# Two preactivation convolutions over 8 images: 32x32 array tiles, four quarters of one image at a time, in place of 64x64 tiles on pairs of images

## The chip, the cores and the metric

The kernel runs on one core of a Trainium2 chip. The metric is the device time of one execution in microseconds. Three runs of the kernel before took 4153.45, 4162.24 and 4164.72 us, so its median is 4162.24 us.

## The reference

The input is `x`, 8 images of 8 channels of 1024 x 1024 float32 (33.6 MB an image). Two layers of the same form follow each other:

```
x = x + conv3x3(groupnorm(x), L0_weight) + L0_bias
x = x + conv3x3(groupnorm(x), L1_weight) + L1_bias
```

The group norm has 4 groups of 2 channels, its mean and variance run over both channels and all rows and columns of one image, with eps 1e-5 and no affine part. The convolution has 8 input and 8 output channels, stride 1 and a border of one zero around the normalised image. Both layers stay in float32.

## The kernel before

**The idea.** The kernel never writes a normalised image. It multiplies the taps by 1/std of the input channel's group, adds the identity to the middle tap (that is the `x +` of the reference), puts what the mean contributes into the bias, and fills the border with the mean, which is zero once normalised. So a layer is one convolution with weights that are made anew for every image, after its mean and variance are known. The result of layer 0 goes to a scratch tensor in HBM, `mid`, and layer 1 reads it back.

**The tiling.** The contraction runs over rows and channels at once: a band matrix maps 8 input rows x 8 channels (64 partitions) to 6 output rows x 8 channels. Horizontal taps are three matmuls that read the same rows shifted by a column (`kw`), added up in PSUM. The TensorE array is used as four 64x64 tiles. In layer 0 (`convolve`, line 620 and on) the two halves of the partitions hold two images and the two column groups two bands of 6 rows; in layer 1 it is the other way round. Neighbouring bands overlap by two rows, so layer 0 loads 8 rows for every 6 that it computes; in layer 1 the overlap is copied inside SBUF by GpSimd (line 405) and ScalarE (line 508).

**The work.** A unit is 12 rows of two images: 24 program matmuls of 512 columns, each of which stands in the trace as two pairs of weight load and matmul (33,232 matmul records; 32,832 of them for the convolutions, from 16,416 in the program). A window is one layer of one pair of images: 85 units and a last one of 4 rows. There are 8 windows, in the order of pairs and layers 0/0, 1/0, 0/1, 2/0, 1/1, 3/0, 2/1, 3/1, so that between the two layers of a pair another pair's window is at work. Of each window 56 units run in a loop (7 trips of 8 units), the others are written out.

**Who does what.** SyncE loads `x` a second time, in pieces of 1 MB, for its statistics (line 270), for the first pair ahead of everything and for the others beside the windows. VectorE takes `bn_stats` of these pieces (L700) and of layer 0's results (L710), makes the weights, and in layer 1 adds the bias to half of the results (L727). ScalarE takes the results out of PSUM (L465, L470) and issues the loads of a unit eight units ahead (L479 from `x`, L492 from `mid`). GpSimd issues the stores (L371 to `mid`, L385 to the output) and copies halo rows. A unit may start when its rows and borders are in SBUF and the results of two units earlier have left PSUM; a result may be written to `out_tile` when the store of four units earlier has landed.

## Time and profile before

| | |
|---|---|
| median of 3 runs | 4162.24 us (4153.45 to 4164.72) |
| span of the profiled execution | 4141.6 us; its time outside the span is not shown; the median run is 20.6 us above the span |
| TensorE matmul busy | 3666.7 us, 89%, 33,232 records |
| VectorE, ScalarE, GpSimd busy | 2025.6, 1762.8, 1360.0 us |
| mean granted TensorE clock | 0.983 |
| moved by DMA | 1435.04 MB, 346 GB/s over the span |
| first convolution matmul | 228.1 us after the start |

The span is one profiled execution. Busy time is the union of an engine's instructions. Four matmuls are at work on the four tiles at the same time, so the mean of one (598 ns) is not what one costs. The DMA row counts the share of time in which the 16 DMA engines had a packet under way, also where that packet waited for memory, so a 9 there does not say that no more bytes could pass; the GB/s row does.

### The profile page before, as it was taken

To read this page: it belongs to the slowest core of one execution; us is meant where nothing else is said; L and a number is where in the kernel's file an instruction comes from. 1 tells how busy PE (TensorE), PEld (TensorE's weight loads), DVE (VectorE), ACT (ScalarE), POOL (GpSimd) and SP (SyncE) were. 2 spreads that over 40 slices of the span, in tenths; PEclk is the share of its full clock that TensorE was granted. 3 is DMA by queue.
4 is the path that set the end of the run, shared out by engine and by line. 5 is a ranking of instruction groups with operands and counts; after the bars stand their busy time and mean duration, and the time that the engine had idled before them with its cause. 6 is when DMAs were issued, how large, how long until landed. Compare 5 with 4: busy or idle time off the path is not lost.

```text
span 4141.6 us, 88712 instructions
## 1 busy us (share of the span) xinstructions
PE 3666.7 (89%) x33232; PEld 1715.4 (41%) x33232; DVE 2025.6 (49%) x3110; ACT 1762.8 (43%) x1381; POOL 1360.0 (33%) x1829
## 2 busy tenths in 40 slices
PE   0087777898889999999888999999999999999999
PEld 0032222353334433354333443345444444566665
DVE  6866666665556344446656444444445322232222
ACT  0032222343334555543333555544443555555554
POOL 0011111121112555531111455552111455555555
PEclk9999998999999999999999999999999999999999
DMA  9989999999999999999999999999999999999997
GB/s 333 396 291 393 386 374 371 366 368 387 382 382 331 331 367 385 380 318 391 390 388 384 305 357 371 374 295 368 362 355 333 291 306 306 306 287 304 305 303 237
DMA packets 367109, 1435.04 MB, mean 346 GB/s; under 512 B 49888, under 2 KB 50016, under 8 KB 334176
## 3 DMA queue, kind: packets, MB, share of 16 engines
q10 hardware_dynamic: 176736, 627.30, 47.9%
q0 software_dynamic: 153344, 536.96, 34.5%
q1 hardware_dynamic: 36864, 268.45, 16.9%
q8 instruction: 119, 1.95, 0.2%
q14 instruction: 46, 0.38, 0.0%
HBM read 895.64 MB, written 536.87 MB: 346 GB/s over the span
## 4 chain that ended last, share of the span: by engine, by line
PE 56%; DMA 15%; ACTq 11%; issue 10%; DVE 5%; ACT 2%; DVEq 0%; POOL 0%; POOLq 0%; SPq 0%
PE conv L653 56%; DMA out_dram<-out_tile 12%; ACTq L479 11%; DMA stat_tile<-x_dram 2%; DVE bn_x L700 2%; ACT out_tile L465 1%; DVE bn_mid L710 1%; DMA mid_dram<-out_tile 1%; DVE out_tile L727 1%; DVE mv_mid L738 1%; DVEq L700 0%; DVE mv_x L732 0%; PE conv L555 0%; ACTq L461 0%; PE conv L583 0%
## 5 line engine op out<-in xcount | busy, mean ns | idle before, releaser
L653 PE MATMUL conv<-x_tile,wts 64*64 64x512 f32 x32832 | 3648.7, 598 | 235.5 <-ACT out_tile L465 140.4
L653 PEld LDWEIGHTS conv<-x_tile,wts 64*64 64x64 f32 x32832 | 1694.9, 134 | 2170.3 <-issue 2037.0
L465 ACT ACTIVATE out_tile<-conv,bias 128x1024 f32<-128x1024 f32 x688 | 728.6, 1110 | 1340.5 <-PE conv L653 791.1
L710 DVE BATCH_NORM_STATS2 bn_mid<-out_tile 128x512 f32 (+1 forms) x1376 | 849.3, 680 | 881.1 <-ACT out_tile L465 880.9
L727 DVE TENSOR_SCALAR out_tile<-conv,bias 128x1024 f32<-128x1024 f32 x340 | 436.4, 1284 | 1168.7 <-PE conv L653 856.7
L371 POOL DMA_DIRECT2D mid_dram<-out_tile x680 | 343.4, 507 | 1708.1 <-ACT out_tile L465 1641.4
L470 ACT ACTIVATE out_tile<-conv,bias 128x1024 f32<-128x1024 f32 x344 | 383.1, 1114 | 764.4 <-PE conv L653 505.6
L508 ACT ACTIVATE x_tile<-x_tile 16x2048 f32<-16x2048 f32 x340 | 648.6, 1908 | 44.9 <-issue 31.6
L700 DVE BATCH_NORM_STATS2 bn_x<-stat_tile 128x512 f32 (+1 forms) x1024 | 628.7, 678 | 45.6 <-DMA stat_tile<-x_dram 45.5
L405 POOL COPY x_tile<-x_tile 16x2048 f32<-16x2048 f32 x340 | 639.1, 1880 | 1.7
L385 POOL DMA_DIRECT2D out_dram<-out_tile x680 | 348.3, 514 | 823.7 <-DVE out_tile L727 758.8
L555 PE MATMUL conv<-share,average 128*128 128x8 f32 x32 | 5.5, 281 | 227.4 <-DVE share L746 222.3
L555 PEld LDWEIGHTS conv<-share,average 128*128 128x128 f32 x32 | 4.8, 215 | 233.3 <-issue 221.5
L396 POOL COPY x_tile<-pad 128x4 f32<-128x4 f32 x64 | 12.2, 198 | 173.2 <-DVE pad L821 172.1
L522 ACT ACTIVATE root<-var 128x8 f32<-128x8 f32 x8 | 1.7, 208 | 137.3 <-DVE var L790 137.2
L738 DVE BATCH_NORM_AGGREGATE mv_mid<-bn_mid 128x2 f32<-128x12 f32 (+1 forms) x24 | 40.1, 1698 | 0.0
L522 ACT ACT_TABLE_LOAD x1 | 1.3, 1283 | 84.5 <-issue 84.5
L732 DVE BATCH_NORM_AGGREGATE mv_x<-bn_x 128x2 f32<-128x192 f32 x32 | 29.9, 983 | 0.0
L335 POOL TENSOR_SCALAR own_group<-same_group 128x4 f32<-128x4 f32 x2 | 0.4, 188 | 44.0 <-DMA rows<-taps_dram 43.9
L379 POOL DMA_DIRECT2D out_dram<-out_tile x16 | 7.8, 495 | 13.4 <-ACT out_tile L470 13.4
L592 PEld LDWEIGHTS conv<-taken,band 64*64 64x64 f32 x144 | 7.2, 134 | 2.2 <-issue 2.2
L583 PE MATMUL conv<-taken,band 64*64 64x1 f32 x144 | 5.5, 208 | 2.7 <-DVE taken L818 2.7
(62 smaller groups left out, 114.5 us busy)
## 6 DMA issues: line engine op xcount, KB each, us to landing
x_tile<-x_dram ACTq DMA_DIRECT2D x680, 512.0 KB, 23.0
stat_tile<-x_dram SPq DMA_DIRECT2D x256, 1024.0 KB, 9.8
out_dram<-out_tile POOLq DMA_DIRECT2D x680, 384.0 KB, 7.8
mid_dram<-out_tile POOLq DMA_DIRECT2D x672, 384.0 KB, 9.3
x_tile<-mid_dram ACTq DMA_DIRECT2D x340, 640.0 KB, 6.4
x_tile<-mid_dram ACTq DMA_DIRECT2D x344, 128.0 KB, 8.5
mid_dram<-out_tile POOLq DMA_DIRECT2D x8, 416.0 KB, 10.0
x_tile<-x_dram ACTq DMA_DIRECT2D x8, 256.0 KB
```

What stands on the lines that cost most here:

```text
L371: pool.dma_start(mid[win.image + i, bass.ds(unit.n * OUT_ROWS + (CH - extra), OUT_ROWS + extra), :], out_tile[VALID - extra:VALID + OUT_RO ...
L385: pool.dma_start(pair[:, bass.ds(row, ROWS_OUT), :], out_tile[VALID:VALID + OUT_ROWS, slot, band]) \
L405: pool.tensor_copy(x_tile[0:PAIR, unit.slot, :, 1:SIDE + 1], x_tile[HALF:HALF + PAIR, earlier.slot, :, 1:SIDE + 1]) \
L465: last = act.activation(out_tile[0:parts, slot, i], conv[0:parts, bank, i], ACT.Identity, bias=bias0[0:parts, win.parity, int(unit.last), ...
L470: last = act.activation(out_tile[:, slot, 0], conv[:, bank, 0], ACT.Identity, bias=bias1[:, win.parity, unit.kind:unit.kind + 1])
L479: act.dma_start(x_tile[:, slot, band, 1:SIDE + 1], rows.rearrange("n c r w -> (n c) r w")) \
L508: act.activation(x_tile[HALF + HALF // 2:HALF + HALF // 2 + PAIR, unit.slot, :, 1:SIDE + 1], x_tile[HALF // 2:HALF // 2 + PAIR, unit.slot, ...
L653: last = nc.tensor.matmul(to, weights, x_tile[HALF * half:HALF * (half + 1), slot, middle, c + kw:c + kw + BANK], start=(kw == 0), stop=(k ...
L700: last = dve.bn_stats(bn_x[:, bass.ds(t * STAT_PARTS + q, 1), :].rearrange("p a b -> p (a b)"), stat_tile[:, s, q * BANK:(q + 1) * BANK])
L710: last = dve.bn_stats(bn_mid[0:parts, unit.win.pair % 2, i, bass.ds(unit.n * 2 + h, 1), :] .rearrange("p a b -> p (a b)"), out_tile[0:part ...
L727: dve.tensor_scalar(out_tile[:, slot, 1], conv[:, bank, 1], bias1[:, win.parity, INNER:INNER + 1], None, ALU.add) \
L738: return dve.bn_aggr(mv_mid[:, region, i, :], bn_mid[:, of.pair % 2, i, first:end, :] .rearrange("p a b -> p (a b)"))
```

## The change

It is a rewrite of the tiling with the same arithmetic idea.

- The array is used as sixteen 32x32 tiles. The four row groups of 32 partitions hold the same rows of four quarters of one image (256 rows each), 4 rows x 8 channels in a partition group. The four column groups are four successive blocks of 4 output rows. The loaded rows are shifted by one against the computed rows, so an output block of 4 rows needs its own block of 4 loaded rows and the next one, and no row is loaded twice.
- An output block is therefore six matmuls (two parts, MAIN and NEXT, by three `kw`) of 32x32 weights. Each row group adds up in a PSUM bank of its own; half the columns (512) of a unit fill four of the eight banks.
- A unit is now 16 rows of each quarter, 64 rows in all: 192 program matmuls. There are 16 units a layer of one image, 256 in the whole kernel (49,152 program matmuls).
- Layers 0 and 1 of an image follow each other directly, and images are taken one by one. Only the next image's statistics run beside the current image. Layer 1 begins with the statistics of all of layer 0's results.
- Image 0 and image 7 are written out, images 1 to 6 run in a loop whose body is a whole image.
- GpSimd issues all loads of `x` (16 of 128 KB a unit) and all stores of the output (16 of 128 KB a unit). SyncE issues the stores to `mid` (4 of 512 KB), the loads from it (4 of 512 KB) and the statistics' loads. ScalarE issues none and takes all results out of PSUM, four banks at a time. No halo is copied.
- `x_tile` and `out_tile` are rings of 4 units of 2 MB each.

The sizes, and in `STATS_0` and `STATS_1` which of the next image's 32 statistics pieces are loaded beside which unit:

```diff
-X_RING = 8
...
-PAIRS = IMAGES // 2
...
+QUARTERS = 4
+QUARTER = SIDE // QUARTERS
+TILE = P // QUARTERS
+BLOCKS = 4
+BLOCK_ROWS = 4
+UNIT_ROWS = BLOCKS * BLOCK_ROWS
+UNITS = QUARTER // UNIT_ROWS
...
+X_RING = 4
...
+STATS_0 = ((0, 1, 2, 3), (4,), (5,), (6, 7), (8,), (9,), (10,), (11, 12), (13,), (14,), (15,),
+           (16,), (17,), (18,), (19,), (20,))
+STATS_1 = ((21,), (22,), (23,), (24,), (25,), (26,), (27,), (28,), (29,), (30,), (31,),
+           (), (), (), (), ())
```

SyncE, one image:

```diff
+            def image(n):
+                win, after = Window(0, n), Window(1, n)
+                for u in range(UNITS):
+                    stats_of_next(win, u)
+                    store_mid(win, u)
+                    first = u - (UNITS - X_RING)
+                    if first >= 0:
+                        sp.wait_ge(stored[0][first % RING], stores_through(win, first))
+                        load_mid(after, first)
+                for s in range(RING):
+                    sp.wait_ge(stored[0][s], stores_through(win, UNITS - RING + s))
+                load_edge(after)
+                for u in range(UNITS):
+                    stats_of_next(after, u)
+                    if u + X_RING < UNITS:
+                        sp.wait_ge(conv_done, HALVES * (after.g + u + 1))
+                        load_mid(after, u + X_RING)
...
```

GpSimd, the loads of `x` and the units of layer 1:

```diff
+            def load_x(n, u):
+                for j in range(BLOCKS):
+                    for q in range(QUARTERS):
+                        row = QUARTER * q + UNIT_ROWS * u + BLOCK_ROWS * j - 1
+                        if row >= 0:
+                            pool.dma_start(x_tile[TILE * q:TILE * (q + 1), u % X_RING, j, 1:SIDE + 1],
+                                           x_block(n, row)).then_inc(rows_loaded[0][u % X_RING], 16)
...
+                for u in range(UNITS):
+                    store_out(after, u)
+                    if not after.last_image and u >= UNITS - X_RING:
+                        load_x(n + 1, u - (UNITS - X_RING))
+                        if u == UNITS - 2:
+                            pool.wait_ge(pad_known, after.w + 2)
+                            pool.sem_inc(results_seen)
+                            load_edge(n + 1)
+                            for s in range(X_RING - 1):
+                                write_pads(0, s)
+                if not after.last_image:
+                    write_pads(0, X_RING - 1)
+                    load_tail(n + 1)
```

TensorE (inside the loop over the two halves `c` of the columns and the two parts), and ScalarE, which takes four banks at a time:

```diff
-                        for half in range(1 if unit.last and win.layer else 2):
-                            for middle in range(1 if unit.last and not win.layer else 2):
...
-                                last = nc.tensor.matmul(
-                                    to, weights,
-                                    x_tile[HALF * half:HALF * (half + 1), slot, middle,
-                                           c + kw:c + kw + BANK],
-                                    start=(kw == 0), stop=(kw == KW - 1))
...
+                        for kw in range(KW):
+                            at = c * BANK + kw
+                            for j in range(BLOCKS):
+                                here = u * BLOCKS + j + part
+                                for q in range(QUARTERS):
+                                    rows = slice(TILE * q, TILE * (q + 1))
...
+                                    last = nc.tensor.matmul(
+                                        conv[TILE * j:TILE * (j + 1), c, q],
+                                        wts[rows, win.layer, part, kw], moving,
+                                        start=(part == MAIN and kw == 0),
+                                        stop=(part == NEXT and kw == KW - 1))
...
+                act.activation(out_tile[:, slot, :, c * BANK:(c + 1) * BANK], conv[:, c],
+                               ACT.Identity, bias=bias[:, win.layer:win.layer + 1]) \
+                   .then_inc(evicted, 1)
```

On TensorE, at the start of the first window, before (`x_loaded3` is the slot of the ring that holds the rows of the unit after the current one, `evicted_a` says that a result has left PSUM):

```order
L653 MATMUL conv<-x_tile,wts 64x512 [waits x_loaded2,pads_written]
L653 MATMUL conv<-x_tile,wts 64x512 x7
L653 MATMUL conv<-x_tile,wts 64x512 [waits evicted_a]
L653 MATMUL conv<-x_tile,wts 64x512 x15
L653 MATMUL conv<-x_tile,wts 64x512 [waits x_loaded3,pads_written]
L653 MATMUL conv<-x_tile,wts 64x512 x7
L653 MATMUL conv<-x_tile,wts 64x512 [waits evicted_a]
```

And the same place now:

```order
L534 MATMUL conv<-x_tile,wts 32x512 [waits x_loaded2,pads_written]
L534 MATMUL conv<-x_tile,wts 32x512 x47
L534 MATMUL conv<-x_tile,wts 32x512 [waits evicted]
L534 MATMUL conv<-x_tile,wts 32x512 x95
L534 MATMUL conv<-x_tile,wts 32x512 [waits evicted]
L534 MATMUL conv<-x_tile,wts 32x512 x47
L534 MATMUL conv<-x_tile,wts 32x512 [waits x_loaded3,pads_written]
```

24 matmuls of 64 rows stood between two waits for loaded rows, now 192 of 32 rows do.

On GpSimd, at the end of layer 1 of the first image and the beginning of the next, now (before, GpSimd issued two stores a unit there and loaded nothing):

```order
L309 DMA out_dram<-out_tile 8x4x1024 x208
L322 DMA x_tile<-x_dram 32x1x1024 x15
L309 DMA out_dram<-out_tile 8x4x1024 x16
L322 DMA x_tile<-x_dram 32x1x1024 x16
L309 DMA out_dram<-out_tile 8x4x1024 x16
L322 DMA x_tile<-x_dram 32x1x1024 x16
L327 TENSOR_SCALAR x_tile<-zeros,own_mean 32x1024
L332 DMA x_tile<-x_dram 8x1024 x3
L352 COPY x_tile<-pad 128x4x2 x3
L309 DMA out_dram<-out_tile 8x4x1024 x16
L322 DMA x_tile<-x_dram 32x1x1024 x16
```

The next image's border rows and pads (L332, L352) stand behind the stores of units 12 to 14 and the loads of the next image's units 0 to 2.

## Rows read from the trace of the kernel before

**Rows 1.** The page: busy time of the engines, and their shares in 40 slices.

```profile
PE 3666.7 (89%) x33232; PEld 1715.4 (41%) x33232; DVE 2025.6 (49%) x3110; ACT 1762.8 (43%) x1381; POOL 1360.0 (33%) x1829
...
PE   0087777898889999999888999999999999999999
...
GB/s 333 396 291 393 386 374 371 366 368 387 382 382 331 331 367 385 380 318 391 390 388 384 305 357 371 374 295 368 362 355 333 291 306 306 306 287 304 305 303 237
```

**Rows 2.** Waits of TensorE: total us, times, longest.

```profile
PE conv L653 <- ACT out_tile L465: 140.4, 64, 5.0
PE conv L653 <- DMA x_tile<-x_dram: 41.5, 31, 2.9
PE conv L653 <- DVE out_tile L727: 39.3, 31, 3.1
```

**Rows 3.** Windows: PE, PEld, DVE, ACT, POOL busy, clock, DMA share, GB/s.

```profile
0.00:120.00 120.00, 0.00 (x0) 0.00 (x0) 76.10 (x126) 1.28 (x1) 6.86 (x41) 1.00 1.00 330
120.00:218.00 98.00, 0.00 (x0) 0.00 (x0) 94.70 (x152) 0.00 (x0) 0.00 (x0) 1.00 1.00 411
300.00:740.00 440.00, 346.60 (x2820) 124.81 (x2816) 283.46 (x471) 122.86 (x116) 59.57 (x118) 0.91 1.02 382
1880.00:2240.00 360.00, 318.02 (x2835) 128.84 (x2829) 216.40 (x358) 124.97 (x118) 60.04 (x120) 0.98 1.03 388
3360.00:3620.00 260.00, 260.00 (x2424) 122.96 (x2422) 64.69 (x51) 151.54 (x101) 146.83 (x151) 1.00 1.00 306
3580.00:3770.00 190.00, 190.00 (x1778) 117.14 (x1773) 64.76 (x86) 107.59 (x73) 105.28 (x118) 1.00 0.97 295
```

**Rows 4.** Timeline of weight loads, three places: start us, length us, count.

```profile
2000.70 0.18 PEld L653 LDWEIGHTS conv<-x_tile,wts 64*64 64x64 f32 x4 [0.25 <-issue]
2001.13 0.18 PEld L653 LDWEIGHTS conv<-x_tile,wts 64*64 64x64 f32 x4 [0.25 <-issue]
...
725.20 0.33 PEld L653 LDWEIGHTS conv<-x_tile,wts 64*64 64x64 f32 x8 [6.41 <-issue]
...
804.33 0.94 PEld L583 LDWEIGHTS conv<-taken,band 64*64 64x64 f32 x32 [0.30 <-issue]
```

**Rows 5.** Timeline at the start: the sums, then the first convolution.

```profile
220.38 0.17 DVE L746 COPY share<-mv_x 128x8 f32<-128x8 f32 x1
...
228.06 4.21 PE L653 MATMUL conv<-x_tile,wts 64*64 64x512 f32 x20 [0.68 <-DVE bias L846]
```

**Rows 6.** Groups by form: busy us, mean ns of one, idle before.

```profile
L700 DVE BATCH_NORM_STATS2 bn_x<-stat_tile 128x512 f32 x928 | 569.7, 678 | 45.6 <-DMA stat_tile<-x_dram 45.5
L738 DVE BATCH_NORM_AGGREGATE mv_mid<-bn_mid 128x2 f32<-128x1020 f32 x8 | 37.9, 4743 | 0.0
L732 DVE BATCH_NORM_AGGREGATE mv_x<-bn_x 128x2 f32<-128x192 f32 x32 | 29.9, 983 | 0.0
L465 ACT ACTIVATE out_tile<-conv,bias 128x1024 f32<-128x1024 f32 x680 | 720.2, 1110 | 1334.2 <-PE conv L653 784.8 <-issue 481.1 <-DMA mid_dram<-out_tile 45.0
```

**Rows 7.** Timeline of GpSimd: transfers issued back to back, loop and end.

```profile
3003.34 1.10 POOL L371 DMA_DIRECT2D mid_dram<-out_tile  x2 [3.96 <-ACT out_tile L465]
...
4135.05 1.95 POOL L379 DMA_DIRECT2D out_dram<-out_tile  x4 [4.02 <-ACT out_tile L470]
```

**Rows 8.** DMA issues of the page: count, KB each, median us to landing.

```profile
x_tile<-x_dram ACTq DMA_DIRECT2D x680, 512.0 KB, 23.0
out_dram<-out_tile POOLq DMA_DIRECT2D x680, 384.0 KB, 7.8
...
x_tile<-mid_dram ACTq DMA_DIRECT2D x344, 128.0 KB, 8.5
```

**Rows 9.** Instruction queue: in 1360 to 1362 us, then in 3580 to 3770.

```profile
q8 instruction: 1, 0.02, 3.9%
...
q8 instruction: 15, 0.25, 0.6%
```

More of the change, by code:

```diff
@@ L11 @@
 P = 128
-HALF = P // 2
 CH = 8
@@ L296, in _ @@
+            for i in range(STAT_SLOTS):
+                load_stat(0, i, None)
+            for i in range(STAT_SLOTS, STATS):
+                load_stat(0, i, i + 1 - STAT_SLOTS)
+            image(0)
+            with sp.Fori(1, IMAGES - 1) as n:
+                image(n)
+            image(IMAGES - 1)
+            last = Window(1, IMAGES - 1)
             for s in range(RING):
-                sp.wait_ge(stored[s], 32 * len(range(s, len(WINDOWS) * UNITS, RING)))
-            sp.wait_ge(stored_last, 16 * last_stores(len(WINDOWS)))
+                sp.wait_ge(stored[1][s], stores_through(last, UNITS - RING + s))
@@ new lines, in store_out @@
+            def store_out(win, u):
+                slot = u % RING
+                pool.wait_ge(evicted, HALVES * (win.g + u + 1))
+                pool.sem_inc(results_seen)
+                for q in range(QUARTERS):
+                    for j in range(BLOCKS):
+                        row = QUARTER * q + UNIT_ROWS * u + BLOCK_ROWS * j
+                        pool.dma_start(out[bass.ds(win.n, 1), :, row:row + BLOCK_ROWS, :]
+                                       .rearrange("n c r w -> (n c) r w"),
+                                       out_tile[TILE * j:TILE * (j + 1), slot, q]) \
+                            .then_inc(stored[1][slot], 16)
@@ L433, in _ @@
+            for u in range(X_RING):
+                load_x(0, u)
+            pool.wait_ge(pad_known, 1)
+            pool.sem_inc(results_seen)
+            load_edge(0)
+            for s in range(X_RING):
+                write_pads(0, s)
+            load_tail(0)
+            image(0)
+            with pool.Fori(1, IMAGES - 1) as n:
+                image(n)
+            image(IMAGES - 1)
         @block.scalar
@@ L549, in _ @@
+            take_root(0)
+            images(act, window)
         @block.tensor
         def _(pe):
-            def mean_sum(n, bank):
-                pe.wait_ge(mean_share, n + 1)
-                regions = 1 if WINDOWS[n].layer == 0 else 3
-                for region in range(regions):
-                    last = nc.tensor.matmul(conv[:, bank, 1, BANK:BANK + BOTH], average[:, :],
-                                            share[:, region], start=(region == 0),
-                                            stop=(region == regions - 1))
-                last.then_inc(mean_summed, 1)
@@ L560, in var_sum @@
-            def var_sum(n, bank):
-                pe.wait_ge(var_share, n + 1)
-                regions = 1 if WINDOWS[n].layer == 0 else 3
-                for region in range(regions):
-                    last = nc.tensor.matmul(conv[:, bank, 1, BANK:BANK + BOTH], average[:, :],
-                                            share[:, region], start=(region == 0),
-                                            stop=(region == regions - 1))
-                last.then_inc(var_summed, 1)
-            def own(i):
-                return slice(VALID * i, VALID * i + HALF)
```

1062 lines of the change are left out of this document (409 added, 653 removed).

## The prediction

> **What bounds the kernel now.** I first read the page's busy times and slices [rows 1]. TensorE is at work 89% of the span, and after the first twentieth, in which nothing but statistics is loaded, at 7 to 9 tenths. So TensorE sets the pace, but not alone: where its slices show 7 or 8, the GB/s row stands near 390, and where they show 9 throughout, at the end, near 305. The windows [rows 3] say the same in numbers. From 3360 to 3620 us TensorE is busy all 260 us at 306 GB/s; from 300 to 740 us only 346.6 of 440 us at 382 GB/s, from 1880 to 2240 us 318 of 360 at 388. The waits [rows 2] name the cause: 140.4 us for results that ScalarE could not take out because `out_tile` was not yet stored, 41.5 us for rows of `x`. I read from it that about 385 GB/s is what the mix of loads and stores gives, and 411 GB/s what pure loading gives (120 to 218 us). Both resources are thus nearly used up, and a change has to relieve both.
>
> Weight loads [rows 4] show the period of the array: four of them every 0.43 us at full clock, one for each tile. 32,832 records in fours are 8,208 periods, 3530 us of the 3649 that the convolutions take.
>
> **TensorE after the change.** 49,152 program matmuls, two records each, are 98,304; sixteen tiles at a time make 6,144 periods. A period streams the same 512 columns, so 0.43 us: 2642 us, or 10.3 us for each of the 256 units. That is 890 us less. The trace of before never has more than four tiles at work, so this has bounds. Below: 10.3 us. Above: no gain from more than four tiles, 41 us a unit. Two rows speak for the lower end. After a wait eight weight loads and their first matmuls go out within 0.33 us, and 32 weight loads of the bias sums pass in 0.94 us, 29 ns each [rows 4]; sixteen pairs at 29 ns are 0.47 us. I take 10.3 to 11.3 us a unit; it turns out not to matter, because of the next paragraph.
>
> **DMA after the change.** An image is 33.6 MB. It is read for its statistics, read for layer 0, written to and read from `mid`, and written out: 5 x 33.6 x 8 = 1342 MB, where 1435 MB moved before. At 385 GB/s that alone is 3486 us, so DMA is now the bound, and I sum by stages, for the images 0 to 6:
> - Layer 0: `x` for units 4 to 15 (25.2 MB), stores to `mid` (33.6), 21 of 32 statistics pieces (22.0), the first four units' rows of `mid` (8.4) are 89.2 MB, 232 us at 385 GB/s [rows 3], 14.5 us a unit, against 10.3 on TensorE.
> - From layer 0 to layer 1 nothing else can run on TensorE. Last results out: 1024 elements take 1110 ns, I put 2048 at 2.0; four `bn_stats` at 0.68 are 2.7; one aggregate of 768 elements at 4743/1020 ns each is 3.6 [rows 6]; from the shares to the first convolution 7.7 us [rows 5]. Sum 16 us. DMA still has stores and loads of its own in part of it, but stays nearly idle in unit 0 too, as loads wait for a slot and stores for results. I take 20 us for both.
> - Layer 1, units 0 to 11: 25.2 MB from `mid`, 25.2 stored, 11.5 of statistics, 61.9 MB, 161 us.
> - From unit 12 on GpSimd is the bound. Two issues stand 1.10 us long, four short ones 1.95 us [rows 7]: 0.49 to 0.60 us a transfer, I take 0.59. Behind unit 12's result stand 48 stores, 48 loads and 3 border rows before the next image may begin: 99 x 0.59 = 58 us, 4 us to land, and unit 12 itself 10.3: 72 us. TensorE would be through in 41.
>
> Sum 232 + 20 + 161 + 72 = 485 us, seven times 3395. The last image has no statistics beside it: 67.1 MB, 174 us; 16; sixteen units of TensorE, 165; the last result, 16 issues and the landing [rows 8], 19. Sum 374.
>
> The start: 32 pieces in place of 64 before the first matmul. 33.6 MB and 8.4 MB of `x` are 102 us at 411 and 127 us at 330 GB/s; VectorE needs 87 us for its 128 `bn_stats` [rows 3, 6]. I take 109, and 12 for four aggregates and the 7.7 us above: 121, where 228 stood [rows 5].
>
> 121 + 3395 + 374 = 3890 us. ScalarE (two results a unit, 4 us of 14.5) and VectorE (eight `bn_stats` on results and some five on pieces a unit of layer 0, 9 us) are hidden under the transfers; the halo copies that go were not waited for [rows 2] and give nothing.
>
> **Instructions.** Most of the program is now written out inside a loop as long as an image. In a stretch of before without a loop, 15 blocks came in for 1778 matmuls and as many weight loads [rows 3, 9]: 0.25 MB, 69 bytes an instruction. 196,608 of them are 13.6 MB. Spread evenly over the DMA engines this is 35 us. A block is one packet, and one took 3.9% of 16 engines x 2 us, 1.25 us, while data went beside it [rows 9]; alone, at 411/16 GB/s, it would need 0.64. If all blocks pass through one engine, it has 96 x 0.64 us more to do an image, of which 84 fall where DMA is the bound: 54 us an image, 409 in all. The bounds are 0 and 409; I take 35: the trace does not tell through how many engines the blocks come, and the lower end is the one that needs no assumption on it. That gives 3925 us of span, against 4141.6. The median of the runs lies 20.6 us above the profiled span; 3925 + 21 is some 3945 us.
>
> **The rivals.**
> - *The array does not hold sixteen tiles at once* (slower). If eight are at work, 12,288 periods are 5284 us, and with start and changes of layer some 5550. It decides from the point where a unit on TensorE passes 14.5 us, 0.60 us a period. For it: nothing before ran more than four. Against it: the pairs of matmul and load were never the limit. Chance 0.12.
> - *One DMA engine carries the instructions* (slower). 3890 + 409 + 21 = 4320 us. For it: the packet of 1.25 us. Chance 0.15.
> - *Small transfers cost bandwidth* (slower). 4144 transfers of 128 KB or less on GpSimd replace 680 of 384 KB and 680 of 512 KB [rows 8]. The stages at the rate are 7 x 393 + 174 = 2925 us; at 85% of 385 GB/s they are 516 more, 4460 us. It is no gain from 358 GB/s down. Against it: the 128 KB transfers of rows 8; for it: they were an eighth of the bytes there, and each now touches a quarter of the partitions. This is what the skill's rule would come to here. Chance 0.08.
> - *DMA does better* (faster). 411 GB/s, 0.49 us an issue and 16 us between layers: 217 + 16 + 151 + 63 = 447 an image, 3129, with 359 for the last, 114 for the start and 33 for instructions 3635, 3655 us with the 21. Chance 0.13.
>
> **How the numbers follow.** The forecast, 3945 us, has 0.52; its own range, from some of the bounds above together, is 3720 to 4160. The range of 3640 to 4400 us leaves out the first rival and parts of the others. Within 0.3% of 4162 us, 4150 to 4175, which is about what a measurement can tell from no change, I put 0.05, from the upper edge of the forecast and the lower edge of the instruction case. Faster: 0.13 + 0.50 = 0.63. Slower: 0.12 + 0.15 + 0.05 = 0.32.
>
> **What would show it.** Right: 98,304 convolution matmul records; weight loads in sixteens every 0.43 us where TensorE does not wait; GB/s near 385 in layer 0; TensorE idle some 30 us at the end of each layer 1 with GpSimd issuing transfers 0.59 us apart, and 16 us between the layers of an image; waits of TensorE for results and rows. Wrong: a period above 0.6 us with TensorE busy throughout, GB/s under 358 in layer 0 while TensorE waits, gaps in TensorE that no semaphore ends, or issues on GpSimd of 0.8 us and more, which would bound layer 1 by themselves.

## The result, and the profile after

The changed kernel takes 5419.41 us (median of four runs, 5397.79 to 5427.39); the kernel before, on the same chip, 4159.84. It is slower by 30%: the ratio is 1.3039, with a 95% interval of 1.2998 to 1.3081. I had forecast 3945 us and a range up to 4400. The profiled execution has a span of 5396.3 us, at a mean granted TensorE clock of 0.877.

The page of the changed kernel: busy times, four rows of the 40 slices, and two lines of its DMA queues (packets, MB, share of 16 engines).

```profile
PE 3837.9 (71%) x99200; PEld 2205.0 (41%) x99200; DVE 1380.8 (26%) x2413; ACT 1011.2 (19%) x529; POOL 2327.4 (43%) x4279
...
PE   0776777767677776767767677776776767767677
...
PEclk9988889988899788988889888888888988889888
DMA  9888989889798897988978889789897988867786
GB/s 346 276 267 234 263 246 305 262 224 258 229 297 267 242 253 233 294 262 228 259 229 294 258 235 268 232 279 268 230 262 226 292 255 242 234 213 245 194 220 189
...
q1 hardware_dynamic: 186016, 808.54, 50.8%
...
q8 instruction: 787, 12.89, 1.0%
```

Against [rows 1]: TensorE is at 6 to 7 tenths nearly throughout, and no engine is at its end: GpSimd has 43%, ScalarE 19%. The DMA engines' row stands mostly at 8 and 9, but where the transfers passed up to 396 GB/s before, they now pass 189 to 305 after the first slice. The instruction queue brought 787 blocks where it brought 119.

The waits of the changed kernel (total us, times, longest).

```profile
ACT out_tile L421 <- PE conv L534: 4137.7, 511, 39.6
PEld conv L534 <- issue: 2365.4, 2237, 34.2
...
PE conv L534 <- issue: 1039.7, 435, 6.1
...
PE conv L534 <- DMA x_tile<-x_dram: 216.5, 8, 33.3
```

In [rows 2] TensorE waited for results and for rows. Here it waits 1039.7 us for nothing that a semaphore shows, 435 times, some 2.4 us each. ScalarE waits for TensorE, 4137.7 us in all. The timeline of TensorE's matmuls in layer 1 (start, length, count) shows the form of it.

```profile
982.73 4.63 PE L534 MATMUL conv<-x_tile,wts 32*32 32x512 f32 x127 [1.37 <-issue]
987.66 4.60 PE L534 MATMUL conv<-x_tile,wts 32*32 32x512 f32 x126 [0.30 <-issue]
994.18 4.46 PE L534 MATMUL conv<-x_tile,wts 32*32 32x512 f32 x128 [1.92 <-issue]
1001.77 4.63 PE L534 MATMUL conv<-x_tile,wts 32*32 32x512 f32 x127 [3.13 <-issue]
1006.89 4.58 PE L534 MATMUL conv<-x_tile,wts 32*32 32x512 f32 x126 [0.49 <-issue]
```

TensorE runs for 4.5 us, 128 matmuls, and stops; again 128, and stops. 128 matmuls and their 128 weight loads are 256 instructions, and a packet of the instruction queue is 12.89 MB / 787 = 16.4 KB, 64 bytes for each of 256. So it looks as if TensorE stood at the end of a block until the next one has come. The times of the blocks' packets say the same: of the 463 stops of more than 0.3 us, 414 end between 1.1 and 1.8 us after such a packet has landed, and these are 1035 us. The packets of that queue start a median of 6.47 us apart (the middle half 4.63 to 7.58), where [rows 9] had 15 in 190 us. My list of what would show the prediction wrong had "gaps in TensorE that no semaphore ends"; these are they.

### The profile page after: what moved, and what is told of

It reads as the page before. It is cut to its first block, busy times and chain, and to the rows that moved or that the text cites. A ratio compares the mean times of both kernels' runs of the same rounds, so it can differ in the third digit from the quotient of the medians.

```text
span 5396.3 us, 219091 instructions
## 1 busy us (share of the span) xinstructions
PE 3837.9 (71%) x99200; PEld 2205.0 (41%) x99200; DVE 1380.8 (26%) x2413; ACT 1011.2 (19%) x529; POOL 2327.4 (43%) x4279
## 3 DMA queue, kind: packets, MB, share of 16 engines
q8 instruction: 787, 12.89, 1.0%
## 4 chain that ended last, share of the span: by engine, by line
PE 64%; issue 26%; DMA 5%; POOL 2%; DVE 1%; ACT 1%; SPq 1%; POOLq 0%; DVEq 0%
PE conv L534 64%; DMA stat_tile<-x_dram 2%; DMA x_tile<-mid_dram 1%; POOL out_dram L309 1%; POOL x_tile L322 1%; DMA x_tile<-x_dram 1%; DMA mid_dram<-out_tile 1%; ACT out_tile L421 1%; POOL x_tile L327 0%; DVE bn_x L704 0%; SPq L185 0%; POOLq L309 0%; DVE mv_mid L598 0%; POOLq L322 0%; SPq L196 0%
## 5 line engine op out<-in xcount | busy, mean ns | idle before, releaser
L534 PE MATMUL conv<-x_tile,wts 32*32 32x512 f32 x97536 | 3790.5, 662 | 1284.8 <-issue 1038.5
L534 PEld LDWEIGHTS conv<-x_tile,wts 32*32 32x32 f32 x97536 | 2149.8, 108 | 2874.8 <-issue 2356.1
L421 ACT ACTIVATE out_tile<-conv,bias 128x2048 f32<-128x2048 f32 x512 | 1007.5, 1968 | 4148.1 <-PE conv L534 4137.7
L309 POOL DMA_DIRECT2D out_dram<-out_tile x2048 | 1103.2, 541 | 1318.1 <-ACT out_tile L421 723.2
L322 POOL DMA_DIRECT2D x_tile<-x_dram x2040 | 1085.7, 551 | 976.5 <-PE conv L534 623.0
L577 DVE BATCH_NORM_STATS2 bn_x<-stat_tile 128x6 f32<-128x512 f32 x896 | 551.6, 680 | 2096.4 <-DMA stat_tile<-x_dram 2096.4
L584 DVE BATCH_NORM_STATS2 bn_mid<-out_tile 128x6 f32<-128x512 f32 x1024 | 631.4, 680 | 1153.4 <-ACT out_tile L421 1153.2
L534 PE MATMUL conv<-tail_tile,wts 32*32 32x512 f32 x768 | 114.4, 619 | 1.2 <-issue 1.2
L704 DVE BATCH_NORM_STATS2 bn_x<-stat_tile 128x512 f32 x128 | 78.8, 680 | 15.0 <-DMA stat_tile<-x_dram 14.3
L337 POOL TENSOR_SCALAR tail_tile<-zeros,own_mean 128x1026 f32<-128x1026 f32 x16 | 46.6, 2912 | 0.0
```

The costliest lines, as they stand in the source:

```text
L309: pool.dma_start(out[bass.ds(win.n, 1), :, row:row + BLOCK_ROWS, :] .rearrange("n c r w -> (n c) r w"), out_tile[TILE * j:TILE * (j + 1), ...
L322: pool.dma_start(x_tile[TILE * q:TILE * (q + 1), u % X_RING, j, 1:SIDE + 1], x_block(n, row)).then_inc(rows_loaded[0][u % X_RING], 16)
L337: pool.tensor_scalar(tail_tile[:, :], zeros[:, :], own_mean[:, layer:layer + 1], None, ALU.add).then_inc(tail_filled, 1)
L421: act.activation(out_tile[:, slot, :, c * BANK:(c + 1) * BANK], conv[:, c], ACT.Identity, bias=bias[:, win.layer:win.layer + 1]) \
L534: last = nc.tensor.matmul(conv[TILE * j:TILE * (j + 1), c, q], wts[rows, win.layer, part, kw], moving, start=(part == MAIN and kw == 0), s ...
L577: last = dve.bn_stats(bn_x[:, i * STAT_PARTS + q, :], stat_tile[:, s, q * BANK:(q + 1) * BANK])
```

## The experiments

Two theories stood at the start. **Refill**: TensorE's program is written out and runs through 256 instructions in some 4 us, and the next 16 KB take longer than that to come when data transfers are under way. **Transfers**: the data's transfers, now smaller, have become slow, and TensorE's stops follow from that. The expectations call them A and C; B is that sixteen tiles are slow on the array by themselves. "Resident" below means that the loop's body stays in the engine's instruction memory and is not fetched again. Where no ratio stands beside a time, it is a single run; thirteen runs of the kernel before on one chip lie within 0.9% of each other.

The first three kernels differ among themselves only in TensorE's instruction stream. So that a loop can have the same addresses in each pass, their matmuls read one fixed tile; TensorE's waits for rows are moved to ScalarE, and SyncE and GpSimd reload a slot when ScalarE has taken the result. `still_flat` is the control, with the stream written out. The loop covers units 2 to 15 of layer 0 and 2 to 11 of layer 1; the other units stay written out.

```diff
-                                        moving = x_tile[rows, here // BLOCKS % X_RING,
-                                                        here % BLOCKS, at:at + BANK]
+                                    moving = still[rows, here % BLOCKS, at:at + BANK]
...
+                with pe.Fori(0, (end - first) // 1) as k:      # still_loop1; // 2 in still_loop2
+                    for j in range(1):
+                        convolve(win, k * 1 + (first + j))
```

> The changed kernel with one thing altered: the convolution matmuls read one fixed tile of rows in place of the rows that were loaded (so the output is not the convolution of x), and ScalarE, not TensorE, waits for the rows before it takes a result out. All transfers, all 98,304 matmul records and the written-out program stay. It is the control for the next two. Every theory expects 5420 us, within 3%, and instruction blocks of 16 KB every 6.5 us (median), 787 of them. If it is far from that, the fixed rows or the moved wait matter by themselves and the next two must be read against it.

> The same, but TensorE's units 2 to 15 of layer 0 and 2 to 11 of layer 1 are a loop with one unit as its body (768 instructions, 49 KB), as large as the loop of the kernel before. Theory A, the arrival of instruction blocks bounds TensorE: the blocks fall from about 787 to under 300, the gaps of TensorE that nothing ends disappear inside the loops, and the time falls to what the transfers allow, 3900 to 4200 us (the forecast's sum of stages). Theory B, sixteen tiles are slow on the array by themselves: the time stays above 5200 us and the period of sixteen stays. Theory C, the small transfers are slow: the time stays above 5000 us with TensorE waiting for results and GB/s near 250.

> The same with two units as the loop's body (1536 instructions, 98 KB). Theory A with a buffer for instructions of at least 98 KB: as with one unit, blocks under 300. Theory A with a smaller buffer: each trip fetches its 6 blocks again, some 700 blocks in all and 5400 us. Theories B and C expect no difference to the body of one unit.

Measured: 5250.93, 4578.89 and 4670.33 us, with 791, 258 and 324 blocks. The control is 3.1% faster than the changed kernel, just outside what was expected of it, but keeps the waits (1099.2 us in 481). The loop of one unit removes most of them and gives back 672 us. Blocks and waits are as the refill theory has them; the time is above its range of 3900 to 4200 us, so something else is missing too. A body of two units, 98 KB, is still resident. Some waits of `still_loop1`:

```profile
ACT out_tile L441 <- DMA x_tile<-x_dram: 873.5, 70, 21.4
...
ACT out_tile L441 <- DMA out_dram<-out_tile: 419.7, 33, 20.3
PE conv L534 <- ACT out_tile L441: 410.5, 64, 12.8
...
PE conv L534 <- issue: 261.7, 126, 5.0
```

TensorE now waits for results, and through ScalarE for rows of `x` and for stores. The version is still 10% slower than the kernel before.

**Blocks and transfers, alone.** `refill_phases` runs only TensorE's stream, written out, 24 blocks in each of five phases, beside different loads.

> Only TensorE's written-out instruction stream (no convolution of x, no output): five phases of 8 units (24 blocks of 16 KB each), with beside them: nothing; 1 MB loads by SyncE as fast as they go; 128 KB loads by GpSimd; both; nothing. Theory A1, a block takes long to come because it queues behind the data: about 3.5 us a block with nothing beside it (the array's own pace, 8 periods of 0.43 us), 6 us and more with loads. Theory A2, the way of a block is long by itself: 6 us and more also in the first and last phase. Theory B, the array is slow: the same in all phases, without gaps between blocks.

Windows of it: PE, PEld, GpSimd busy, clock, DMA share, GB/s.

```profile
16.00:106.00 90.00, 90.00 (x2867) 70.63 (x2847) 0.00 (x0) 1.00 0.02 4
110.00:228.00 118.00, 89.86 (x2566) 47.28 (x2561) 0.00 (x0) 0.99 0.96 394
236.00:345.00 109.00, 105.71 (x3139) 61.68 (x3120) 84.12 (x159) 1.00 0.72 191
350.00:500.00 150.00, 110.19 (x2870) 55.70 (x2850) 42.64 (x81) 0.92 0.98 322
548.00:635.00 87.00, 87.00 (x2752) 67.40 (x2734) 0.00 (x0) 1.00 0.02 4
```

The median time from one block's packet to the next is, in this order, 3.87, 6.11, 4.43, 6.96 and 4.08 us. Without data traffic the blocks come as fast as TensorE uses them and it never stops, so 3.9 and 4.1 us are its own pace and not the shortest that a block can take. Beside loads it stops after nearly every block, 18 of 20 in the second window and 21 of 22 in the fourth. At a DMA share of 0.72 it hardly does (3.2 us in all). A block's own packet takes 1.1 to 1.2 us in every phase, so the packet itself is not what grows; where the rest of a block's 6 to 7 us passes, the trace does not show. This is the refill theory, with no convolution's data behind it.

**The other side.** If a slower stream does not outrun its blocks, writing out the loop of the kernel before must be free.

```diff
-                in_order(pe, win, step)
+                for b in range(HEAD):
+                    step(Unit(win, b), None)
+                for k in range(TRIPS):
+                    for j in range(X_RING):
+                        step(Unit(win, HEAD + j, k), (j, k))
+                for b in range(TAIL, STEPS):
+                    step(Unit(win, b), None)
```

> The kernel before with TensorE's inner loop written out, as the changed kernel has it; nothing else changes. Its stream is 8 instructions in 0.43 us, so a block of 256 lasts 13.8 us. If a block takes 6 to 7 us to come under data traffic (the microbenchmark: 6.1 and 7.0 us an interval, 3.9 alone), it is always there in time: within 1% of the kernel before, some 250 to 380 blocks in place of 119, and no more time of TensorE in waits that nothing ends. If writing a stream out costs by itself, whatever its pace (an instruction fetched costs a fixed time): two thirds of the 196,608 instructions, so two thirds of the 670 us that the resident loop gave back, some 4600 us.

Measured: 4180.27 us, ratio 1.0019 (0.9994 to 1.0045), with 267 blocks a median of 14.2 us apart. There are more than twice the blocks, no time is lost that the interval could tell from nothing, and TensorE's waits that nothing ends are 4.3 us in all. What costs is the pace, not the writing out.

**Less data beside it.** `light_stats` is the changed kernel with 235 MB of statistics loads left out; VectorE reads 64 columns of a piece in place of 512 with it.

```diff
-                sp.dma_start(stat_tile[:, s],
+                sp.dma_start(stat_tile[:, s, 0:256],
```

> The changed kernel with an eighth of the statistics: each piece of 1 MB is a load of 128 KB (128 partitions by 1 KB) and VectorE reads 64 columns in place of 512. Everything else, TensorE's written-out stream included, is as in the changed kernel. 235 MB less are moved. If the changed kernel is bound by the wait for instruction blocks, which lasts longer when more data is in flight: a stage goes to what the last image, which has no statistics, shows already (276, 220 and 57 us where the others have 297, 230 and 67), 35 us an image, and the start falls by some 80 us: 5050 to 5150 us. If it is bound by the bytes at the 253 GB/s that it moves: 235 MB less are 930 us less, 4490 us. If the blocks' wait has nothing to do with data in flight: only the start falls, 5330 us.

Measured: 5211.6 us. 54 us of the 208 are at the start; an image falls from 664 to 643 us, not by the 35 I expected, and a block still comes a median of 6.15 us after the last. The time lies between the second range and the 5330 us of no effect. Bytes alone were not the bound: 4490 us is far off. How much longer a block takes does not go down in proportion with the traffic.

**A loop in the real computation.** `resident` computes everything: units 0 to 11 of a layer are three trips of four units.

```diff
+                with pe.Fori(1 if first else 0, UNITS // X_RING - 1) as k:
+                    for j in range(X_RING):
+                        convolve_looped(win, j, k)
+                for u in range(UNITS - X_RING, UNITS):
+                    convolve(win, u)
```

> The whole computation. The changed kernel with units 0 to 11 of each layer as a loop of three trips over four units (3,072 instructions, 196 KB; in the first layer of image 0, units 4 to 11) and units 12 to 15 written out as they are. If a body of 196 KB stays resident, as one of 98 KB did, half of the units' blocks go: 400 to 440 blocks in place of 787, and about half of the 671 us that the resident one-unit loop gave against the changed kernel's 5250 with the fixed tile: 5050 to 5150 us. If it does not stay, 790 blocks and 5400 to 5440 us.

Measured: 5557.31 us, ratio 1.3332 (1.3292 to 1.3372), with 839 blocks. 196 KB do not stay: there are 52 more blocks than in the changed kernel, and the ratio is 1.3332 in place of 1.3039. The bound lies between 98 and 196 KB. `x_tile` is a ring of four units, and with its addresses fixed in the body a trip is four units. A shorter body for the real computation was not tried.

**What is left: 569 us an image.** Times of a stage, from ScalarE's results, mean of images 1 to 6, in us; layer 1 begins with the change of layer. A stage ends with its last result, so TensorE's wait at the change of image, 30 us in the changed kernel, is in its layer 0, while the forecast has it in its 72.

| | layer 0 | layer 1, to unit 11 | units 12 to 15 | image | last image |
|---|---|---|---|---|---|
| forecast, without instructions | 232 | 181 | 72 | 485 | 374 |
| changed kernel | 332 | 264 | 67 | 664 | 629 |
| still_flat | 320 | 258 | 66 | 644 | 603 |
| still_loop1 | 270 | 228 | 71 | 569 | 469 |
| loop1_third | 279 | 215 | 49 | 543 | 443 |

First the array. `period` is TensorE alone, in a resident loop.

> TensorE alone, no transfers, no other engine; five phases of 25 units, each a loop whose body is one unit (so that instructions are fetched once a phase): sixteen tiles (4 column groups by 4 row groups); eight (2 by 4); four (1 by 4); eight (4 by 2); sixteen again. A unit is 12 steps, each with two periods. If the array takes sixteen tiles at the pace of four, 0.43 us a period, a unit is 10.3 us in every phase, 258 us a phase. If sixteen pairs of load and matmul take longer to give out than 512 columns to pass, which is what 12.0 us a unit in the last image of the resident version says: some 290 to 300 us in the phases with sixteen, 258 in those with eight and four. If 12.0 us came from waits for results and the clock there: 258 in all.

Measured, per period: 0.516 us with sixteen tiles, 0.430 with eight (two column groups), 0.430 with four, 0.430 with eight (four column groups), 0.511 with sixteen. Four of the windows (PE, PEld, GpSimd busy, clock, DMA share, GB/s):

```profile
30.00:300.00 270.00, 270.00 (x8493) 210.94 (x8474) 0.00 (x0) 1.00 0.00 0
330.00:560.00 230.00, 230.00 (x4296) 94.67 (x4287) 0.00 (x0) 1.00 0.00 0
600.00:830.00 230.00, 230.00 (x2148) 81.58 (x2144) 0.00 (x0) 1.00 0.00 0
850.00:1080.00 230.00, 230.00 (x4296) 126.17 (x4288) 0.00 (x0) 1.00 0.00 0
```

The array does take sixteen tiles at once, but the period of 32 instructions is then 0.51 us: a unit is 12.3 us, not 10.3. Whether handing out the instructions is what costs the 0.08 us, no run shows.

Then the transfers. `loop1_third` leaves out two taps of three, and so two thirds of TensorE's work.

```diff
-                        for kw in range(KW):
+                        for kw in (0,) if part == MAIN else (KW - 1,):
```

> The version whose TensorE loop is resident (4578.9 us) with one tap in three: 2 steps of sixteen tiles a half in place of 6, so 4 us of TensorE a unit in place of 12.3. The transfers, the statistics and the other engines' work are the same. If transfers alone set the 256 us of layer 0 and the 185 us of units 0 to 11 of layer 1: both stay, only the change of layer loses some 8 us and the last image some 80: 4400 to 4500 us. If it is TensorE at 12.3 us a unit that meets uneven transfers and loses what it has not made up: layer 0 falls to 230 us or less, layer 1 to 165, and the whole to 4000 to 4150 us.

Measured: 4341.39 us. That is between the two ranges. With TensorE at 36%, layer 0 stays as long as it was (279 us against 270) and layer 1 up to unit 11 nearly so (215 against 228), and the waits have gone to the transfers; only units 12 to 15 fall from 71 to 49. The waits of it, then two of its windows (PE, PEld, DVE, ACT, GpSimd, clock, DMA share, GB/s): layer 0 of the first and of the last image.

```profile
PE conv L534 <- ACT out_tile L441: 2248.7, 199, 45.3
...
ACT out_tile L441 <- DMA x_tile<-x_dram: 1557.0, 110, 45.9
ACT out_tile L441 <- DMA out_dram<-out_tile: 1087.4, 77, 23.3
```

```profile
120.00:350.00 230.00, 95.13 (x2034) 41.58 (x2034) 118.96 (x207) 56.08 (x30) 111.75 (x205) 0.70 1.01 344
...
3920.00:4120.00 200.00, 85.84 (x1856) 37.16 (x1856) 77.82 (x125) 59.49 (x31) 124.14 (x231) 0.70 1.02 330
```

In these windows the DMA engines are busy all the time at 330 to 344 GB/s, where the kernel before passed 382 to 388 at the same share [rows 3]. So with a third of TensorE's convolution work the change still takes 4341 us, 4% more than the whole kernel before. That is not the transfers alone: the changes of layer and GpSimd's issues at the end of an image are in it too.

**Why not 385 GB/s?** Three edits of `still_loop1`, in what I held possible: where the loads read, how large they are, and who issues them.

```diff
-                                           x_block(n, row)).then_inc(rows_loaded[0][u % X_RING], 16)
+                                           x_rows[bass.ds((n * UNITS + u) * (QUARTERS * P) + TILE * (BLOCKS * q + j), TILE), :])
```

> The version whose TensorE loop is resident (4578.9 us); the loads of x are the same in number, size, queue and target, but each reads 128 KB in one piece (32 whole rows that follow each other) in place of four rows of each of eight channels, 4 MB apart. The data read is not used. If the lower transfer rate (330 GB/s in layer 0 where I put 385) comes from where the loads read, layer 0 falls from 256 us an image to 225 to 235 and the whole to 4300 to 4400 us. If it comes from the size of the transfers or from GpSimd's queue: within 1% of 4579.

Measured: 4549.61 us. Layer 0 falls from 270 to 253 us, but layer 1 up to unit 11 grows from 228 to 238, so an image is only 9 shorter. In all it is 0.6%, less than runs of one kernel differ. So it is not where the loads read, or that is only a small part.

```diff
-                            pool.dma_start(x_tile[TILE * q:TILE * (q + 1), u % X_RING, j, 1:SIDE + 1],
-                                           x_block(n, row)).then_inc(rows_loaded[0][u % X_RING], 16)
+                    pool.dma_start(x_tile[low:P, u % X_RING, q, 1:SIDE + 1],
+                                   x[bass.ds(n, 1), :, row:row + (P - low) // CH, :]
+                                   .rearrange("n c r w -> (n c) r w"))
```

> The version whose TensorE loop is resident (4578.9 us), with 4 loads of x a unit of 512 KB each onto 128 partitions, sixteen rows of eight channels, the form of the kernel before, in place of 16 of 128 KB onto 32 partitions. The data read is not used; the stores stay. If 128 KB is too small for the rate (the third rival of the prediction): layer 0 back to 385 GB/s, 225 us an image in place of 256, and units 12 to 15, where GpSimd then issues 76 transfers in place of 112, from 71 to 50: 4200 to 4300 us. If the loads' size costs nothing, or even helps as in the measurement of transfers alone (346 GB/s beside 1 MB loads against 272 for 512 KB): layer 0 stays at 256 us or is longer, only units 12 to 15 gain: 4430 to 4600 us.

Measured: 4732.61 us, slower, though GpSimd is busy 1541.1 us in place of 2327.7. Larger loads are worse here.

```diff
+                    if win.layer == 0 and u + X_RING < UNITS:
+                        load_x(act, win.n, u + X_RING)
+                    if win.layer == 1 and not win.last_image and u >= UNITS - X_RING:
+                        load_x(act, win.n + 1, u - (UNITS - X_RING))
```

> The version whose TensorE loop is resident (matmuls read one fixed tile, 4578.9 us), with the 16 loads of x a unit issued by ScalarE behind its second result instead of by GpSimd. GpSimd keeps the stores to out and the border rows. If what is left of the miss, 85 us an image over the forecast, is GpSimd's work (its issues in units 12 to 15, 71 us where TensorE needs 48, and its queue's share of DMA time in layer 0): layer 0 falls from 256 us an image to 225 or less, units 12 to 15 to 50, in all 4150 to 4300 us. If 128 KB transfers cost bandwidth by their size, DMA stays at 320 to 330 GB/s in layer 0 and only units 12 to 15 gain: 4400 to 4480 us. If TensorE itself sets 12 us a unit and the rest is waits for mid: no more than 1% faster.

Measured: 4811.71 us, slower, which none of the expectations had. The timeline of ScalarE, its results and its issues (start, length, count):

```profile
242.50 1.97 ACT L433 ACTIVATE out_tile<-conv,bias 128x2048 f32<-128x2048 f32 x1 [12.97 <-issue]
...
244.41 18.19 ACTq L178 DMA_DIRECT2D x_tile<-x_dram  x15
262.73 1.97 ACT L433 ACTIVATE out_tile<-conv,bias 128x2048 f32<-128x2048 f32 x1 [16.40 <-issue]
```

An issue holds ScalarE 1.2 us, sixteen of them 19 us, and the next result waits behind them: 1466.3 us of ScalarE's waits end in "issue". ScalarE became a bound of its own, so this run does not answer what it was made for.

`mixes` measured transfers with nothing else beside 1 MB loads of SyncE:

> No convolution, no statistics: transfers alone, in six phases with a barrier after each. In every phase SyncE's queue loads 36 pieces of 1 MB, four in flight; beside it, at most eight in flight: phase 0 nothing; 1 ScalarE's queue, 72 loads of 512 KB onto 128 partitions (the form of the kernel before); 2 ScalarE's queue, 288 loads of 128 KB onto 32 partitions (the form of the change); 3 GpSimd's queue, 72 loads of 512 KB; 4 GpSimd's queue, 288 loads of 128 KB; 5 GpSimd's queue, 288 stores of 128 KB. The output is not computed. Read from it: GB/s while both queues are at work. Small transfers cost bandwidth whoever issues them (the third rival of the prediction): phase 2 as low as phase 4, both some 330, phases 1 and 3 near 400. It is GpSimd's queue that costs, by its many short packets: phase 2 near 400, phases 3, 4 and 5 low. Only small transfers from GpSimd's queue cost: phase 4 and 5 alone low. No such cost: all near 400, and the 321 to 330 GB/s of the resident version has another reason.

Its windows of phases 0 to 5 while both queues run (GpSimd busy, clock, DMA share, GB/s):

```profile
20.00:85.00 65.00, 0.00 (x0) 1.00 1.01 422
120.00:280.00 160.00, 0.00 (x0) 1.00 0.87 250
...
430.00:530.00 100.00, 0.00 (x0) 1.00 0.94 323
...
750.00:890.00 140.00, 8.09 (x14) 1.00 1.02 273
...
1040.00:1130.00 90.00, 23.39 (x44) 1.00 1.02 346
...
1310.00:1370.00 60.00, 18.89 (x35) 1.00 1.02 422
```

No expectation holds. Loads of `x` in blocks of eight channels bring the sum down, the 512 KB ones more (to 250 and 273 GB/s) than the 128 KB ones (323 and 346), on either queue. Small stores cost nothing: 422. Beside the loads SyncE's packets of 8 KB mostly become longer: they take a median of 313 ns alone, 452 and 318 in phases 1 and 2, 481 and 391 in phases 3 and 4, 309 in phase 5. So the third rival's cause, that these transfers are smaller than those of the kernel before, is refuted in both places. What it is in such a load that costs was not taken apart here: `mixes` has none that reads 128 KB in one piece. Why this kernel's mix passes 330 GB/s where the mix before, which had the 512 KB loads too, passed 385 stays open.

## Why the prediction was wrong

- **The step that failed is "Instructions".** I counted the instructions rightly: 196,608, and 12.89 MB came in against my 13.6. But I priced them as bytes that share the DMA engines, 35 us, with an upper bound of 409 from one engine's queue. They cost a wait. The stream uses a block in 8 periods, 4.1 us, and beside the transfers the next takes 6 to 7. Measured with everything else equal: 5250.93 - 4578.89 = 672 us. The pace could be worked out from my own text: some 240 instructions a block, 32 of them every 0.43 us, 3.2 us a block. Of the delivery I had seen only the packet, 1.25 us. The trace of before could not show more, since its blocks came a median of 13.9 us apart because none was needed sooner. I never asked how long a block takes to come, or set pace against delivery.
- **The rate of 385 GB/s, 232 and 161 us a stage.** The engines were fully used, as I said, but passed 330 to 344. By the table, layer 0 of `still_loop1` is 270 us against 232 and the next stage 228 against 181: 84 us an image, some 590 in the seven, and 95 in the last (469 against 374). Not all of it is the rate, as the next point says. The third rival had the size right (85%, 327 GB/s) and the wrong cause: larger loads were slower. Its 4460 us is within 3% of `still_loop1`, which is in part luck, as the changes of layer below are in that time too.
- **The change of layer** was put at 16 us, and at 20 with the transfers' idle time. From ScalarE's last result of layer 0 to the next convolution, `still_loop1` takes 29 to 36 us in the seven images that have statistics beside them, 33 in the mean, and 14.5 in the last, which has none; the changed kernel takes 20 to 27. The interior of my sum was right. What it left out is the order of VectorE's program: the last `bn_stats` of the layer's results stand behind those of a statistics piece, and that piece has not landed. In the seven images they begin 15 to 21 us after the last result, in the last image at once. VectorE's timeline in `still_loop1`, image 2, whose last result is out at 1511.2 us, and then in the last image:

```profile
1526.82 2.47 DVE L585 BATCH_NORM_STATS2 bn_x<-stat_tile 128x6 f32<-128x512 f32 x4 [9.29 <-DMA stat_tile<-x_dram]
1529.21 2.46 DVE L592 BATCH_NORM_STATS2 bn_mid<-out_tile 128x6 f32<-128x512 f32 x4
1531.81 3.62 DVE L606 BATCH_NORM_AGGREGATE mv_mid<-bn_mid 128x2 f32<-128x768 f32 x1
...
4314.42 2.47 DVE L592 BATCH_NORM_STATS2 bn_mid<-out_tile 128x6 f32<-128x512 f32 x4 [3.86 <-ACT out_tile L441]
```

  That is 13 us an image over the 20, some 90 of the 590. No run has the statistics in another order, so what that would give back is not shown.
- **TensorE's 10.3 us a unit** was 12.3. Under transfers of 16.9 us a unit (270 / 16) that changes little: taking two thirds of TensorE's work away gave 26 us an image and 237 in all. The row of 29 ns a pair, 0.47 us for sixteen, was nearer than the end I took. The Trainium skill, "TensorE: Matmul & The Clock Gate", Part 3 (Packing small matmuls), has 10.6 times for sixteen tiles and 3.07 for four, so 3.45 times for sixteen against four. `period` measured 4 x 0.430 / 0.513 = 3.35: the page was nearer than I was. My text puts its figures to bfloat16; the page names no type for them, and here it is float32. The first rival, that the array does not hold sixteen tiles, is refuted by the same run.
- **The second rival**, one DMA engine carrying the instructions, put 54 us an image; the image grew by 75 between `still_loop1` and `still_flat`. Its mechanism, a longer queue at a saturated engine, isn't what the rows show: a block's packet takes 1.1 to 1.2 us at any traffic, also alone, where I had put 0.64, and it is TensorE that waits for it, not the data.
- **GpSimd's bound from unit 12 on** was the right mechanism: TensorE stands some 30 us for it at the end of a middle image, as forecast, in all the 216.5 us of the waits above. The term of 72 us is 94 from unit 11's result to TensorE's next start. Unit 12 takes 21 us in place of 10.3, and the 99 issues with the fill of the border take 71 in place of 58. In image 0, which is written out, they take 58. In the loop most issues stand 0.64 to 0.65 us apart, with some 0.1 us ahead of each in which GpSimd shows nothing, where image 0 has 0.53:

```profile
1371.16 10.13 POOL L309 DMA_DIRECT2D out_dram<-out_tile  x16 [10.61 <-ACT out_tile L421]
...
1394.50 9.49 POOL L309 DMA_DIRECT2D out_dram<-out_tile  x15 [0.15 <-issue]
...
1404.84 9.64 POOL L322 DMA_DIRECT2D x_tile<-x_dram  x15 [0.15 <-issue]
```

  That is GpSimd's timeline in the changed kernel, image 1 (start, length, count).
- **Small terms.** One result takes 1.97 us (put at 2.0), the aggregate 3.62 (3.6). The first result begins at 143 us, where 121 and half a unit, 126, was the forecast: the start was 17 us too short.
- **The chances.** 0.63 for faster rested on the instructions' bounds, 35 to 409 us, whose upper end was itself a sum over bytes. A wait was never priced, so the range could not hold 5419. That the first rival's 5550 us came near is chance, as its cause is refuted.

The account: 3945 forecast; 4579 with the transfers' real rate and the array's real period and the loop resident; 5251 with the stream written out; 5419 with TensorE itself waiting for its rows. Of this last 168 us, 19 are the start (first result at 143 us in place of 124) and most of the rest would be TensorE's 30 us at each change of image: in `still_flat` the row waits are ScalarE's, TensorE computes half a unit ahead, and its longest stop at these changes is 5 us, and 13 before the last image. An image is 20 us shorter there. The split of the 168 us is read from the two traces; no run changes one part alone.

No version beat the kernel before. Of this tiling even the one with a third of TensorE's work did not.

## What to carry to other kernels

Before a loop is written out, compare two times: that in which an engine runs through one instruction block, and that between blocks in a run which is as loaded as the kernel will be and in which the engine stops for them. A trace in which it never stops shows only its own pace. Small tiles make this worse: four 64x64 tiles took 8 instructions in 0.43 us, sixteen 32x32 tiles 32 in 0.51. Do the transfers' sum with the rate of a mix that has the new loads in it, and test "how fast without the other engine's work" first: one run with a third of the matmuls would have shown that the rest of this schedule takes some 4340 us. Where an engine works through two streams in a fixed order, look at which of them the critical one stands behind.

## What the runs showed of the hardware

- A block of 256 TensorE instructions (16.4 KB) came every 3.9 us without data traffic, which was TensorE's own pace, every 4.4 at a DMA share of 0.72, and every 6.1 and 7.0 at 0.96 and 0.98 (`refill_phases`). There TensorE went on a median of 1.4 us after the block's packet had landed. With blocks 14.2 us apart (`before_flat`) it waited 4.3 us in the whole kernel.
- A loop body of 98 KB of TensorE instructions stayed resident (`still_loop2`, 324 blocks), one of 196 KB did not (`resident`, 839).
- Matmuls on 32x32 tiles of 512 columns in float32: four and eight tiles have the same period, 0.430 us, and sixteen 0.51 (`period`).
- A 128 KB load of 32 rows in eight pieces held ScalarE 1.2 us an issue beside other traffic (`still_act`); GpSimd's issue instruction takes 0.55 (the changed kernel).
- SyncE's 1 MB loads passed 422 GB/s alone and beside 128 KB stores, 323 to 346 in sum beside 128 KB loads of eight channels, and 250 to 273 beside 512 KB ones (`mixes`).
- With a third of TensorE's convolution work (`loop1_third`, busy 36%) the granted clock had a mean of 0.683, so the engine stood at the lower of its two levels, 1.2 and 2.4 GHz, for a good part of the time. No run shows what that cost.
